# Moves of the third unit tile by tile, one tile in a place of its own, and two orders changed at the end of an attention kernel

## The reference

```
x = x + 0.5 * moe(layernorm(x))
x = x + attention(layernorm(x))
x = x + 0.5 * moe(layernorm(x))

q = hidden @ Wq.T + bq
scores = q @ memory_keys.T / sqrt(128)
probs = softmax(scores)
attention = (probs @ memory_values) @ Wo.T + bo
```

## Time and profile before

| what | value |
|---|---|
| time, median of 3 runs | 653.56 us (652.54 to 653.99) |
| the profiled execution's own time | 654.36 us |
| its span, first to last instruction | 652.6 us |
| TensorE busy | 612.6 us (94%) |
| VectorE busy | 531.6 us (81%) |
| ScalarE busy | 455.9 us (70%) |
| mean granted TensorE clock | 0.992 |

### The profile page before, as it was taken

One profiled execution on the slowest core, in us unless ns is written; L12 is line 12 of the kernel. 1 busy time (PEld: TensorE's weight loads), 2 busy tenths in 40 slices (PEclk: granted clock), 3 DMA queues, 4 the chain that ended last, 5 costly groups with the idle time before them and its releaser, 6 DMA issues.

```text
span 652.6 us, 9400 instructions
## 1 busy us (share of the span) xinstructions
PE 612.6 (94%) x2868; PEld 432.5 (66%) x2884; DVE 531.6 (81%) x944; ACT 455.9 (70%) x765; POOL 398.3 (61%) x443
## 2 busy tenths in 40 slices
PE   7799998798989999999999999999999988999997
PEld 4455544576767777777777777777777766645543
DVE  5889886886967978988887897897898858699885
ACT  3577787474757777777777776777776765567886
POOL 4987670462565966867677587596677787524100
PEclk9899999899989999999999999999999999999999
DMA  8021210425264373653735727447355360000000
GB/s 308 6 64 34 65 33 1 113 58 137 59 153 102 92 162 86 141 118 81 174 82 129 158 61 170 95 99 171 81 138 109 87 130 1 1 17 17 33 32 33
DMA packets 35857, 59.19 MB, mean 91 GB/s; under 512 B 9056, under 2 KB 9696, under 8 KB 35680
## 3 DMA queue, kind: packets, MB, share of 16 engines
q1 hardware_dynamic: 31936, 53.34, 34.2%
q10 hardware_dynamic: 3360, 4.21, 2.5%
q0 software_dynamic: 512, 1.05, 0.6%
HBM read 8.23 MB, written 2.10 MB: 16 GB/s over the span
## 4 chain that ended last, share of the span: by engine, by line
PE 64%; DVE 19%; issue 5%; ACT 4%; SPq 3%; POOL 2%; DMA 1%; ACTq 1%; DVEq 0%; POOLq 0%
PE banks L1400 7%; PE banks L1402 7%; PE banks L1401 7%; PE banks L1441 6%; PE banks L1443 6%; PE banks L1442 6%; PE banks L1261 4%; DVE bank_max L1123 4%; PE banks L1420 4%; PE banks L1252 4%; DVE probsT L1019 4%; DVE E L1118 3%; SPq L351 3%; PE banks L1451 2%; PE banks L1271 2%
## 5 line engine op out<-in xcount | busy, mean ns | idle before, releaser
L551 POOL TENSOR_TENSOR p_lo<-probsT,p_hi 128x768 fp32r<-128x768 f32 (+1 forms) x128 | 226.9, 1776 | 129.1 <-ACT p_hi L759 128.7
L1123 DVE TENSOR_REDUCE bank_max<-banks 128x1 f32<-128x1024 f32 x128 | 156.0, 1219 | 33.4 <-PE banks L1402 32.4
L1400 PE MATMUL banks<-kv_lo,q_parts 128*128 128x512 f32 x256 | 112.4, 439 | 10.2 <-ACT E L781 5.1
L759 ACT ACTIVATE p_hi<-probsT 128x768 fp32r<-128x768 f32 (+1 forms) x128 | 104.3, 816 | 24.0 <-PE banks L1443 21.1
L1118 DVE STREAM_TRANSPOSE E<-E 128x1024 f32<-128x1024 f32 x92 | 113.5, 1234 | 3.8 <-ACT E L781 3.8
L1019 DVE SCALAR_TENSOR_TENSOR probsT<-banks,E 128x1024 bf16<-128x1024 f32 x80 | 95.3, 1217 | 21.5 <-PE banks L1252 21.4
L781 ACT ACTIVATE E<-banks,neg_max 128x1024 f32<-128x1024 f32 x92 | 102.4, 1113 | 12.6 <-DVE neg_max L1129 6.7
L661 ACT ACTIVATE probsT<-probsT 128x1024 bf16<-128x1024 bf16 x96 | 92.5, 982 | 22.8 <-DVE probsT L1019 18.4
L1441 PE MATMUL banks<-p_hi,kv_lo 128*128 128x512 f32 x256 | 108.1, 422 | 0.3 <-issue 0.3
L1442 PE MATMUL banks<-p_lo,kv_hi 128*128 128x512 f32 x256 | 102.7, 401 | 0.0
L1443 PE MATMUL banks<-p_hi,kv_hi 128*128 128x512 f32 x256 | 102.7, 401 | 0.0
(11 more groups left out here) (128 smaller groups left out, 888.5 us busy)
## 6 DMA issues: line engine op xcount, KB each, us to landing
probsT<-E SPq DMA_DIRECT2D x224, 128.0 KB, 2.4
probsT<-E SPq DMA_DIRECT2D x208, 64.0 KB, 2.0
E<-in_keys_values SPq DMA_DIRECT2D x8, 512.0 KB, 3.5
probsT<-E ACTq DMA_DIRECT2D x64, 64.0 KB, 2.3
out<-X SPq DMA_DIRECT2D x8, 256.0 KB, 2.0
X<-in_x SPq DMA_DIRECT2D x1, 1280.0 KB, 9.4
probsT<-E POOLq DMA_DIRECT2D x16, 64.0 KB, 2.5
X<-in_x SPq DMA_DIRECT2D x3, 256.0 KB, 5.8
```

Source lines behind the costliest of these rows:

```text
L551: pool.tensor_tensor(moved_part(p_lo, ring), moved_pair(ring // UP, ring % UP), moved_part(p_hi, ring).bitcast(fp32), ALU.subtract).then_i ...
L759: act.activation(moved_part(p_hi, ring), moved_pair(ring // UP, ring % UP), ACT.Copy).then_inc(moved_hi_done, 1)
L1123: dve.tensor_reduce(bank_max[:, i % 2, h:h + 1], score_pair(u, i, h).rearrange("p b n -> p (b n)"), AX.X, ALU.max).then_inc(bank_max_done, 1)
L1400: pe.matmul(bank, qh, kl, start=True, stop=False)
```

## The change

1. The moves of unit 2 go as those of unit 1 do: after each tile's block transposes SyncE issues 12 transfers of that tile and ScalarE four, and each tile of units 1 and 2 has a semaphore of its own (`single`). From unit 3 on the batches stay. SyncE issues 36 transfers of 64 KB in unit 2 where it had 16 of 128 KB and 12 of 64 KB. ScalarE issues 12 (four each at H = 20, 22 and 24) where it had four (H = 23).
2. Tile 2 of unit 0 goes to the last 2048 words of the arena `probsT`, which is where tile 2 of unit 1 is moved to. ScalarE no longer waits before unit 1's own tile; the moves of unit 1's tile 2 wait for unit 0's transposes instead (`probsT_done` of 8), on SyncE and on ScalarE.
3. After unit 15 ScalarE does `own_high` before `copy_oT`. This concerns one place, H = 132 with unit 14.
4. TensorE does transposes before values from H = 127 on instead of H = 128.

```
@@ -162,7 +165,8 @@
-        assert at[0] <= 2 * MOVED * BLOCK
+        assert at[0] <= 2 * MOVED * BLOCK - BLOCK
@@ -319,12 +324,14 @@
             if t < MOVED:
-                return probs[:, 1, 0, :] if w == 0 else E2[:, t, :, :].rearrange("p b n -> p (b n)")
+                return (arena[:, 2 * MOVED * BLOCK - BLOCK:] if w == 0 else
+                        E2[:, t, :, :].rearrange("p b n -> p (b n)"))
             return probs[:, w % 2, 0, :]
...
         def move_strip(eng, u, k, tile, count, b, i):
-            eng.dma_start(*strip(u, tile, count, b, i)).then_inc(moved[k], 16)
+            done = single[u - 1][tile] if 0 < u <= SINGLE else moved[k]
+            eng.dma_start(*strip(u, tile, count, b, i)).then_inc(done, 16)
@@ -401,13 +405,16 @@
                 wait(sp, moved_lo_done, UP * (u - 1))
-                if u == 1:
+                if u <= SINGLE:
                     for tile in range(MOVED):
-                        sp.wait_ge(squares_done, squares_of(1) + 2 * (tile + 1))
+                        sp.wait_ge(squares_done, squares_of(u) + 2 * (tile + 1))
+                        if u == 1 and tile == MOVED - 1:
+                            sp.wait_ge(probsT_done, UP)
                         for b in range(QUADS - 1):
                             for i in range(QUADS):
-                                move_strip(sp, 1, second_batch(tile), tile, 1, b, i)
+                                move_strip(sp, u, 0, tile, 1, b, i)
@@ -748,10 +755,13 @@
                 if ring % UP == 0:
-                    for k in range(len(BATCHES)):
-                        wait(act, moved[k], moves(k, ring // UP + 1))
-                if ring == UP:
-                    act.wait_ge(moved[2], 16 * QUADS * QUADS)
+                    w = ring // UP
+                    if 0 < w <= SINGLE:
+                        for done in single[w - 1]:
+                            act.wait_ge(done, MOVE)
+                    else:
+                        for k in range(len(BATCHES)):
+                            wait(act, moved[k], moves(k, w + 1))
@@ -769,11 +779,14 @@
                 if i < MOVED and h == 0:
...
+                    if 2 <= u <= SINGLE + 1:
+                        before = [t for t in range(MOVED) if slot_of(u - 1, t) == slot_of(u, i)][0]
+                        act.wait_ge(single[u - 2][before], MOVE)
@@ -784,8 +797,7 @@
                     if i == MOVED and h == 0:
-                        wait(act, probsT_done, UP if u == 1 else (u - 1) * UP)
+                        wait(act, probsT_done, (u - 1) * UP)
@@ -821,7 +833,7 @@
                     w = projection_at(H + 3)
-                    if w:
+                    if u <= LAST and w:
                         copy_oT(w)
@@ -840,17 +852,24 @@
                         own_high(ring)
+
+                    if u > LAST and w is not None:
+                        copy_oT(w)
...
-                    if H in (HALVES + 4, HALVES + 6, HALVES + 8):
-                        tile = (H - HALVES - 4) // 2
-                        act.wait_ge(squares_done, squares_of(1) + 2 * (tile + 1))
+                    of, at_h = divmod(H - 4, HALVES)
+                    if 1 <= of <= SINGLE and at_h in (0, 2, 4):
+                        tile = at_h // 2
+                        wait(act, moved_lo_done, UP * (of - 1))
+                        act.wait_ge(squares_done, squares_of(of) + 2 * (tile + 1))
+                        if of == 1 and tile == MOVED - 1:
+                            act.wait_ge(probsT_done, UP)
                         for i in range(QUADS):
-                            move_strip(act, 1, second_batch(tile), tile, 1, QUADS - 1, i)
-                    if 1 < u < LAST and h == HALVES - 1:
+                            move_strip(act, of, 0, tile, 1, QUADS - 1, i)
+                    if SINGLE < u < LAST and h == HALVES - 1:
@@ -1505,7 +1524,7 @@
-                    for step in (2, 0) if u > LAST else (0, 2):
+                    for step in (2, 0) if H >= UNITS * HALVES - 1 else (0, 2):
```

19 lines of the change are left out of this document (10 added, 9 removed).

## The result

The changed kernel takes 647.71 us (median of 4 runs, 646.12 to 648.28), the one before 653.55 (4 runs, 652.54 to 653.99). The ratio is 0.9919, 95% interval 0.9894 to 0.9944: 5.84 us less. The forecast was 646.2, range 643.9 to 650.4.

A forecast was written before the change was run, and what follows sets the result against it. TensorE, 94% busy, bounds the kernel, so gains come only where it stands still: 2.1 + 4.45 + 0.5 + 0.5 = 7.55 us, less 0.15 for small holds, 7.4, from 653.56 to 646.2 us; range 643.9 to 650.4.

The forecast's parts named there:

- The two places: ScalarE's waits at the end of unit 1 (157.27) and of unit 2 (189.48); forecast gains 2.1 and 4.45 us.
- signs of being wrong: New transfer wait at H = 26, TensorE hole behind ScalarE's bursts, fallen clock from 150 to 200, or end waits unchanged in sum.
- Part 1: End of unit 1: own tile's exponentials start 2.7 us earlier without their wait; 2.1 us won, between 1.6 and 2.7.
- The moved wait: Unit 1's tile 2 moves start after unit 0's transposes, so unit 2's tile 1 exponentials are held 1.1 us.
- Part 2: Unit 3's first exponentials need one tile instead of two; 2.9 us standing still plus 1.55 for the clock, 4.45 us.
- the hole: TensorE idle 2.66 us before 190.74, at the start of unit 3; forecast to go, between 2.9 and 4.45 us won.
- What part 2 adds: More issues in unit 2, 36 on SyncE and 12 on ScalarE: nothing counted, 1.5 us as bound at H = 26.
- The hold: ScalarE at H = 26 waits for unit 2's last transfer before the first ring's moved high part; some 1.3 us forecast.
- the first rival: Hole moves instead of going, through more issues and the wait at H = 26: 648.2 to 650.8 us, 24 in 100.
- Parts 3 and 4: Copy behind the high part at H = 132, and transposes first at H = 127; 0.5 us won at each.
- No change: Rival: the head's gain is taken back because transfers, not TensorE, bound the middle; 653.5 us, 5 in 100.
- slower: Rival: two issuing engines slow each other, unit 2's last transfer lands late; 660 us at 1.1 an issue, 5 in 100.

The follow-up runs named there:

- first pair of traces: One profiled execution each of the kernel before and the changed kernel; from H = 16 to 26 they take 31.13 and 28.87 us.
- second pair: One more execution each of the kernel before and the changed kernel, profiled later; measured 653.6 and 647.99 us.
- part 1 alone: The kernel before with only the own tile's new place; batches in unit 2 and both orders at the end as before: 649.57 us.
- the kernel with the pair: The changed kernel with tiles 1 and 2 of unit 2 moved together after tile 2: 646.12 us, ratio 0.9894 to the kernel before; once more, 647.52 us.

## Why the prediction was right, and where not

**The two places.** The waits of ScalarE at 157.27 and 189.48 were what held TensorE, and both are gone. The middle of the attention only shifted: -0.2 and 0.8 us over 97 half steps in the two pairs, within the scatter of this stretch. Taken from the start of H = 16, the signs named for the two places came true: ScalarE starts the own tile 2.8 us earlier (2.7 was forecast), and the group of scores that stood at 198.37 starts 6.7 us earlier (6.55). The last scores of the attention come only 4.9 us earlier where 6.5 was forecast, since 1.65 us are lost again between H = 29 and 30; the idle time of 1.42 us at 193.35 and the wait on a transfer at H = 26 are the prediction's own signs of being wrong.

**Part 1, forecast 2.1, between 1.6 and 2.7.** Measured 2.26 over the same place in the first pair of traces, 2.1 by undoing it (30.96 against 28.87 us), and 2.08 in the second pair (30.92 against 28.84). The moved wait did what was said: the exponentials of unit 2's tile 1 are released by a transfer, after 0.41 us instead of 1.1. TensorE feels little of it: up to H = 20 it has won 2.6 us, and up to H = 26 it gives back 0.34.

**Part 2, forecast 4.45 for the hole.** In the two traces that the forecast compares it is 4.46 us. That agreement is partly luck. Its first term, 2.9 us of standing still, is real, with 2.5 us in the second pair of traces (11.76 against 9.26). Its second, "together 1.55 us more than two steps of 3.04; this is what the lower clock cost", is a mis-sized term. The low clock was read from a single execution. The second trace of the same kernel has nearly the same hole, 2.37 us against 2.66, at the full clock, and the two steps behind it take 3.06 and 3.05 us, so the term is nothing there. The lower bound of 2.9 that the prediction kept for it was the better value.

**What part 2 adds, forecast nothing.** This is the step that failed: "TensorE needs the own part nearly two half steps later. I count nothing, with 1.5 us as the bound." The hold on ScalarE was 2.71 and 1.56 us where 1.3 was forecast, and TensorE lost 1.65 and 0.5 us. Two things were wrong in it. The first is the row of issues, priced at 36 x 0.64 = 23.0 us. Counted from the start of H = 16, ScalarE reached the ring after 36.7 us, near the forecast (190.7 - 153.68 = 37.0), but the last transfer landed after 39.25 us and not after 38.3 (192 - 153.68). That 191.56 looks like the 192 of the forecast is due to this trace being 1.37 us ahead. One long issue, 1.79 us, makes most of the difference. The prediction's own rows had it in: the issues from 174.53 to 185.78 came 0.75 us apart on average, not 0.64.

The second is the room, which decides what TensorE loses. At H = 29 the transposes for the next queries stand ahead of the values and wait for the low part of the ring that the hold delays. In a half step without them the part would, as the program reads, have been needed only for the own transposes behind the values; no run shows that. Moving the values ahead does not help either, since the queries' chain is then late. So the first rival happened in part beside the forecast. The bursts of ScalarE's issues cost nothing up to H = 26: the stretch from H = 16 takes 28.87 and 28.84 us with 12 issues and 28.90 with four (part 1 alone), and from 174 to 190 us TensorE is full.

**What the two halves of the head are worth apart.** With part 1 there, moving unit 2 tile by tile gives 0.85 us by the medians, which is not clear of their noise. In the traces it closes a hole worth 2.0 to 2.5 us and opens one of 0.5 to 1.65. Without it the kernel is still 4.28 us faster than the kernel before that ran beside it, so most of the 5.84 us comes from part 1 and from the end. Part 1 also shortens the hole itself a little, 11.10 and 11.62 us from H = 26 to 29 against 11.76 at the full clock.

**Parts 3 and 4, forecast 0.5 and 0.5.** Measured 0.50 and 0.39 by undoing each, 0.86 together. The reasons hold too: the 1.90 us of waiting for a low part come back for the most part one ring later, behind VectorE's routing steps; and the wait for the copied projection is 0.69 us where 0.7 was said.

**The sum.** Forecast 7.4, measured 5.84. With what the runs show in place of the two terms it is 2.1 + 2.5 - 0.5 to 1.65 + 0.9, so 3.9 to 5.0. The medians give at least 0.8 more than that. What makes it up is not shown; the low clock before H = 16, worth about 1 us, the one behind the hole and the scatter of the middle, 1.7 us over the traces, can fall unevenly on so few runs. So that the measured time lies in the forecast's range rests on the mechanisms of both places, but two errors worked against each other in it: about 2 us too much for the hole, 0.5 to 1.65 us too little for the hold.

**The rivals.** "No change" and "slower" did not happen. The slower one named the issue time, with 0.96 us an issue as its condition; over the 36 issues it is 0.68 us in the first trace and 0.65 in the second. That a long row of issues can make the kernel slower is nonetheless so, as the kernel with all units tile by tile shows. The Trainium skill advises to coalesce many small transfers into one ("DMA: Bandwidth & Descriptors", Rules for kernel authors). These traces agree in the form of issues: a transfer of two tiles takes SyncE about as long as a transfer of one, and pairing tiles 1 and 2 won 1.24 us between H = 26 and 30 in the first traces and 0.24 in the second.

## What to carry to other kernels

In this kernel it paid to split a batch of transfers only where somebody waited for its first part, and to keep together what is waited for as a whole: the cost is in the number of issues of the queue, and it falls due at the next wait for the last of them. When a hold is priced at nothing because of the room behind it, go through every instruction that waits for the same bank, the rare ones too, which come only in every second unit. Price a row of issues by the time that such a row took and not by its most frequent step: 0.64 us an issue was used, 0.75 stood in the rows, and 0.68 came. Put two traces on a common start before a forecast time is compared with a measured one. And take no clock of a single execution into the sum: a second trace of the kernel before would have moved the forecast by 1.55 us.

## What the runs showed of the hardware

The granted clock does not always fall behind the same hole of TensorE. After 2.66 us of idle time it was 0.50 at 193 to 194 us in one trace, after 2.37 us in the next trace of the same program it was 1.00. An idle time of 2.2 us just before 120 us is the same in all 14 traces; in six of them the clock then falls to 0.50, and in eight it stays at 1.00. The changed kernel alone shows both.

In a row of SyncE's issues of about 0.6 us each, single ones take 0.96 to 2.05 us. Each of the 14 traces has at least one in unit 2, and no run shows what makes them long.

Two groups of SBUF to SBUF transfers beside each other, 128 KB each 0.64 us from SyncE and four from ScalarE, go with a full share of the transfer engines (0.99 at 229 GB/s from 182 to 186 us in the kernel with the pair), and some of ScalarE's issues take longer in that stretch: two took 1.97 us there against 1.16 to 1.26 with the change.
